# A new order of the first block's side work in a two-layer fp32 kernel

## The reference, cut to what matters

```
feats   = exp(x @ (ab*gs).T - 0.5*|x|^2*ab^2) * AB / sqrt(R)     # random features of 8192 tokens
weights = the same function of input_weights
x1  = layernorm(x + feats @ weights.T)
re  = x1 @ cos(theta + theta_noise);  im = x1 @ sin(phi + phi_noise)
out = layernorm(x1 + sqrt(re*re + im*im))
```

## Time and profile before

| | us |
|---|---|
| median of 3 runs | 774.54 (774.42 to 775.04) |
| the profiled execution | 774.44 |
| its span | 772.6 |
| busy: PE / DVE / ACT / POOL | 750.4 / 496.8 / 373.2 / 179.0 |

### The profile page before, as it was taken

The page is one execution under the profiler, slowest core; times in us unless marked ns, Lnnn a source line. Parts: engine busy times, 40 slices in busy tenths (PEclk is TensorE's granted clock), DMA queues, the critical chain, the costliest instruction groups (busy, mean ns, idle before and its releaser), DMA issues.

```text
span 772.6 us, 10427 instructions
## 1 busy us (share of the span) xinstructions
PE 750.4 (97%) x3396; PEld 617.8 (80%) x3396; DVE 496.8 (64%) x888; ACT 373.2 (48%) x643; POOL 179.0 (23%) x309
## 2 busy tenths in 40 slices
PE   9977989999999999999999999999999999999995
PEld 7855868888888888888888888888888888888884
DVE  4888684847648474674747567474755747576464
ACT  6824926263463616446362644527265462625322
POOL 4966030302112030211203012120201212030222
PEclk9998999999999999999999999999999999999998
DMA  8650050411404032140402214050231405010001
GB/s 277 213 178 0 1 177 1 118 59 46 131 27 149 0 99 78 41 136 21 155 0 79 97 41 136 10 166 1 73 104 41 136 0 162 15 62 6 28 28 54
DMA packets 32750, 60.75 MB, mean 79 GB/s; under 512 B 3168, under 2 KB 3168, under 8 KB 32736
## 3 DMA queue, kind: packets, MB, share of 16 engines
q1 hardware_dynamic: 32736, 60.60, 23.7%
HBM read 43.78 MB, written 16.81 MB: 78 GB/s over the span
## 4 chain that ended last, share of the span: by engine, by line
PE 86%; DVE 7%; ACT 3%; issue 2%; POOL 2%; POOLq 0%; DVEq 0%; ACTq 0%
PE token_ps L502 14%; PE token_ps L504 14%; PE token_ps L503 14%; PE project_ps L491 6%; PE project_ps L493 6%; PE project_ps L492 6%; PE token_ps L554 6%; PE token_ps L552 6%; PE token_ps L553 6%; PE turn_ps L560 3%; DVE stats L730 1%; DVE expo L653 1%; DVE trig L708 1%; DVE trig L712 1%; ACT F_raw L387 1%
## 5 line engine op out<-in xcount | busy, mean ns | idle before, releaser
L306 POOL TENSOR_TENSOR var_eps<-mv,eps 128x1 f32<-128x1 f32 x128 | 41.5, 324 | 568.1 <-DVE mv L734 568.0
L424 ACT ACTIVATE late<-token_ps 128x512 f32<-128x512 f32 x120 | 71.7, 598 | 131.5 <-PE token_ps L504 131.5
L416 ACT ACTIVATE zT_hi<-turn_ps 128x512 fp32r<-128x512 f32 x64 | 38.0, 598 | 182.2 <-PE turn_ps L560 182.2
L491 PE MATMUL project_ps<-xT_hi,gs_hi 128*128 128x512 f32 x248 | 102.1, 412 | 1.0 <-DVE xT_lo L648 0.7
L552 PE MATMUL token_ps<-W_hi,F_hi 128*128 128x512 f32 x256 | 99.7, 389 | 0.0
L554 PE MATMUL token_ps<-W_hi,F_lo 128*128 128x512 f32 x256 | 99.6, 389 | 0.0
L553 PE MATMUL token_ps<-W_lo,F_hi 128*128 128x512 f32 x256 | 99.6, 389 | 0.0
L648 DVE TENSOR_TENSOR xT_lo<-xT_raw,xT_hi 128x512 fp32r<-128x512 f32 x64 | 43.7, 690 | 85.9 <-ACT xT_hi L472 85.5
L493 PE MATMUL project_ps<-xT_hi,gs_lo 128*128 128x512 f32 x248 | 98.0, 395 | 0.0
L492 PE MATMUL project_ps<-xT_lo,gs_hi 128*128 128x512 f32 x248 | 97.4, 393 | 0.0
L745 DVE TENSOR_TENSOR late<-z,late 128x512 f32<-128x512 f32 x64 | 44.2, 691 | 81.9 <-ACT late L457 81.3
(11 more groups left out here) (126 smaller groups left out, 1333.2 us busy)
## 6 DMA issues: line engine op xcount, KB each, us to landing
xT_raw<-in_xT SPq DMA_DIRECT2D x16, 1024.0 KB, 5.9
x_tok<-in_x SPq DMA_DIRECT2D x16, 1024.0 KB, 7.0
out_tokens<-o_tile SPq DMA_DIRECT2D x64, 256.0 KB, 2.0
norm_bc<-token_norms SPq DMA_DIRECT2D x15, 256.0 KB, 3.6
trig<-in_gsT SPq DMA_DIRECT2D x4, 256.0 KB, 4.0
z<-in_wT SPq DMA_DIRECT2D x4, 256.0 KB, 4.7
trig<-in_theta_noise SPq DMA_DIRECT2D x4, 256.0 KB, 6.7
trig<-in_theta SPq DMA_DIRECT2D x4, 256.0 KB, 7.9
```

The costliest lines, as they stand in the source:

```text
L424: nc.scalar.activation(dst, bank[:, :], ACT.Square).then_inc(square_done, 1)
L491: nc.tensor.matmul(o, gs_hi[:, c, cols], rhs_hi[:, c, :], start=(c == 0), stop=False)
```

## The change

GpSimd turns all four tiles of theta and the first of phi ahead of the roots, makes the four roots of block 0 without angle work between them, and turns the second tile of phi behind them. VectorE turns the other two tiles of phi itself, as one tile of double width, and takes over the three sums of squared columns. VectorE splits block 1's columns before it reduces the first two angles. It reduces theta's third and fourth tile between the residuals. ScalarE rounds block 1's columns before it takes the token squares; the third tile's sines come before the first turned tile is rounded, the fourth's after it. At the end of step 0 ScalarE's order is written out, with the four token squares of block 3 last.

```diff
@@ GpSimd
-            a = squares[1]
-            pool.wait_ge(squares_made, C + 2)
-            pool.tensor_tensor(a[0], a[0], a[1], ALU.add).then_inc(block_squares_summed, 1)
...
-            for c in range(3):
-                add_noise(trig, c, theta_loaded, HALF_PI)
-                take_turns(trig, c)
+            for c in range(C):
+                count_turns(trig, c, theta_loaded, HALF_PI)
+            count_turns(late, 0, phi_loaded, 0.0)
...
                 if first:
-                    take_turns(late, 0)
-                    for c in range(1, C):
-                        add_noise(late, c, phi_loaded, 0.0)
-                        take_turns(late, c)
+                    count_turns(late, 1, phi_loaded, 0.0)
@@ ScalarE
+            act.wait_ge(project_done, 2 * C)
+            split_hi(1)
             act.wait_ge(columns_cleared, 1)
             act.wait_ge(x_loaded[1], 16)
             for j in range(C):
                 sum_square(2, j, 1, 0)
-            act.wait_ge(project_done, 2 * C)
-            split_hi(1)
...
-            for c in (0, 1):
+            for c in (0, 1, 2):
                 sine(trig, c, cos_hi, 0)
...
                     round_turned(0)
+                    sine(trig, 3, cos_hi, 0)
                     round_turned(1)
-                    sine(trig, 2, cos_hi, 0)
-                    sine(trig, 3, cos_hi, 0)
...
+                if first:
+                    square(0, 1)
+                    square(1, 1)
+                    magnitude(0)
+                    magnitude(1)
+                    round_columns(0)
+                    square(2, 1)
+                    magnitude(2)
+                    round_columns(1)
+                    square(3, 1)
+                    magnitude(3)
+                    round_columns(2)
+                    round_columns(3)
+                    for j in range(C):
+                        sum_square(b + 3, j, slot, 1 - slot)
+                    return
@@ VectorE
+            a = squares[1]
+            dve.wait_ge(squares_made, C + 2)
+            tt(a[0], a[0], a[1], ALU.add).then_inc(block_squares_summed, 1)
+            dve.wait_ge(squares_made, 2 * C)
+            tt(a[2], a[2], a[3], ALU.add).then_inc(block_squares_summed, 1)
...
+                if n == 1:
+                    dve.wait_ge(block_squares_summed, 2)
+                    tt(a[0], a[0], a[2], ALU.add).then_inc(block_squares_summed, 1)
...
+            def whole_angles(cs):
+                angle, turns = late[:, cs, :], late[:, slice(C + cs.start, C + cs.stop), :]
...
+                tt(angle, angle, turns, ALU.add).then_inc(angle_step, 1)
+                ts(turns, angle, 1.0 / (2 * np.pi), ROUNDER, ALU.mult, ALU.add).then_inc(angle_step, 1)
+                ts(turns, turns, -ROUNDER, -TWO_PI_A, ALU.add, ALU.mult).then_inc(angle_step, 1)
+                tt(angle, angle, turns, ALU.add).then_inc(turns_made, cs.stop - cs.start)
...
+            for c in range(C):
+                split_lo(1, c)
             reduce_angle(trig, 0, 0)
             reduce_angle(trig, 1, 0)
             turn_norms(2, 0)
-            for c in range(C):
-                split_lo(1, c)
...
                     halves(n[j], j, y[:, j % 2, :], y_made, stats, stats_made)
+                    if first and 1 <= j < C - 1:
+                        reduce_angle(trig, j + 1, 0)
...
                 if first:
+                    split_turned(0)
+                norm1(C - 1)
+                if first:
                     exponent(C * (b + 2) + 1, 1, slot, project_ps[1], 1)
                     split_sine(trig, 0, cos_hi, cos_lo, 0, cos_made)
+                    split_sine(trig, 1, cos_hi, cos_lo, 0, cos_made)
                     split_turned(1)
+                    split_sine(trig, 2, cos_hi, cos_lo, 0, cos_made)
+                    reduce_angle(late, 0, C)
                     split_turned(2)
+                    split_sine(trig, 3, cos_hi, cos_lo, 0, cos_made)
                     split_turned(3)
+                    reduce_angle(late, 1, C)
+                    whole_angles(slice(2, 4))
+                    split_sine(late, 0, sin_hi, sin_lo, C, sin_made)
+                    reduce_angle(late, 2, C)
+                    reduce_angle(late, 3, C)
+                    split_sine(late, 1, sin_hi, sin_lo, C, sin_made)
+                    split_sine(late, 2, sin_hi, sin_lo, C, sin_made)
+                    split_sine(late, 3, sin_hi, sin_lo, C, sin_made)
```

## The result

The changed kernel takes 776.44 us (median of 11 runs, 775.54 to 777.97), the kernel before beside it 774.90 (11 runs, 774.42 to 776.22): a ratio of 1.0018, interval [1.0010, 1.0027]. It is slower, as forecast, but by 1.54 us, not by 3.7. The profiled execution has a span of 774.8 us against 772.6.

The account below looks back on a forecast made before the run. Only the opening, one VectorE-ScalarE chain to block 1's first z, was taken to bound the kernel. Tail 4.35 less 0.65 for an earlier last sine gave +3.7 us: 778.2 us, range 774.2 to 781.2.

Parts of the forecast that it names:

- Piece 3: From the last sine to VectorE's last xT_lo: ScalarE's token squares coming last make it 4.35 us later, 1 either way.
- Rival (b): Tail wait hidden, sums of squares slipping in while ScalarE waits for VectorE: total about +1 us, 775.6; chance 0.12.
- Piece 2: From VectorE's first residual to the last sine: less contention and undelayed roots, leaving the last sine 0.65 us earlier than before.
- My 3.9 for the double-width steps: VectorE's four steps on two phi tiles as one, before the last sine: 3.9 us taken, between 2.1 and 4.4.
- The term of 2.8 for GpSimd's one tile: Between first residual and last sine, GpSimd's one remaining tile delays VectorE: four instructions at 0.7 us, 2.8 in all.
- excess of 0.7: Extra us for a VectorE instruction with two SBUF inputs beside GpSimd's work: 1.3 instead of 0.61.
- Piece 1: VectorE up to its first residual: contention with GpSimd's earlier start makes it 5.3 us late, bounds 0 and 9.
- The signs that I had named: Right: splits end near 18.8, last sine near 76.7, block 1's first transpose near 108.5; wrong: last sine before 74.
- Rival (a): The front wins: GpSimd waits at most turns, excess 0.35 for 14 instructions, last sine 71.2, total 773.3; chance 0.15.
- The clock: TensorE's 1.2 GHz stretch after longer idle before block 1's later matmuls: taken as costing 0, bounds 0 and +2 us.
- TensorE's two long waits: TensorE idle 4 to 5 us before its first transpose and about 4 before block 2's projection, the former off the chain.
- The idle after 115: TensorE, once past the opening: no idle after 115 us, named as a sign of being right.

## Why the direction was right and the size wrong

**The bound** was right: only the opening moves the time. From block 1's last transpose on (116.69 before, 118.78 after) the rest of the span is 655.9 to 656.0 us in the kernel before, the changed kernel and all eight experiments: each gain or loss is made ahead of that transpose. All but one were there already at the last xT_lo; only with the transpose moved was what had been gained up to that point lost behind it.

**Piece 3, the tail,** was right: forecast 4.35, measured 4.20, and 4.18 in the kernel before with only this edit. The wait in front of the transpose was expected at about 3 us and is 2.71. It was worked out from program order and durations of the earlier trace rows alone. Rival (b) falls with it: ScalarE waits for the sums (2.34 and 2.40) with the token squares behind them in its list.

**Piece 2 is where the forecast failed most, by the price of contention.** I made it 29.6 us from the first residual to the last sine; it took 28.34. My 3.9 for the double-width steps is what they took (66.69 to 70.61):

```profile
66.69 1.22 DVE L725 TENSOR_TENSOR late<-late 128x1024 f32<-128x1024 f32 x1
67.94 0.69 DVE L728 TENSOR_SCALAR late<-late 128x1024 f32<-128x1024 f32 x1
68.67 0.69 DVE L731 TENSOR_SCALAR late<-late 128x1024 f32<-128x1024 f32 x1
69.47 1.22 DVE L734 TENSOR_TENSOR late<-late 128x1024 f32<-128x1024 f32 x1
```

The estimate by pages of the Trainium skill that I set beside them comes to 3.8, not to the 3.9 that I wrote.

The term of 2.8 for GpSimd's one tile, four instructions at an excess of 0.7, was too large. Only three places beside it stretch, by 0.96 (z, 0.55 alone), 0.41 (two cosine splits, 1.29 alone) and 0.50 (one, 0.68 alone), 1.9 in all, so 0.9 of the error. Another 0.5 is the four rounds of residual, statistics and normalise, which without the stretched z took 7.6 us, not 8.1:

```profile
57.35 1.51 DVE L760 TENSOR_SCALAR z<-y,mv,rstd 128x512 f32<-128x512 f32 x1 [0.36 <-POOL rstd L295]
...
59.45 1.70 DVE L643 TENSOR_TENSOR cos_lo<-trig,cos_hi 128x512 fp32r<-128x512 f32 x2
...
61.67 1.18 DVE L643 TENSOR_TENSOR cos_lo<-trig,cos_hi 128x512 fp32r<-128x512 f32 x1
```

**Piece 1** had the same fault and a smaller error: 5.3 late forecast, 4.57 measured (31.60 less 27.03, each from the first split). The five instructions that follow the first split cost 5.94 − 0.61 = 5.33 us, 1.07 each, not the 1.3 that I took. So VectorE was 1.8 us late behind the loop of exponents and splits, not 2.8. Block 1's splits then took 5.45 against 5.2, and the angle pairs 3.93, inside my 3.2 to 4.2. What I got wrong is that the price has no one value: it goes with what GpSimd has in flight. GpSimd's timeline beside the five:

```profile
15.31 1.79 POOL L270 TENSOR_TENSOR trig<-trig 128x512 f32<-128x512 f32 x1 [2.58 <-DMA trig<-in_theta]
17.18 0.94 POOL L274 TENSOR_SCALAR trig<-trig 128x512 f32<-128x512 f32 x1
18.21 0.93 POOL L277 TENSOR_SCALAR trig<-trig 128x512 f32<-128x512 f32 x1
19.22 0.93 POOL L280 TENSOR_SCALAR trig<-trig 128x512 f32<-128x512 f32 x1
```

Both engines step by the same 1.02 there (GpSimd starts at 17.18, 18.21, 19.22, VectorE's sums at 18.58, 19.60 and the exponents at 20.61). Beside a GpSimd sum (1.3 alone) one VectorE instruction comes to 1.7, as the third sum at 21.93.

Together pieces 1 and 2 erred by 0.7 + 1.3 = 2.0 us and piece 3 by 0.15, which is, to rounding, the distance from +3.7 to +1.52. So the mechanism stood, and the term that failed is the excess of 0.7 us for each contended instruction: it was 0.46 for the five behind the first split, and 1.9 us in place of 2.8 in all beside the one tile of piece 2.

The signs that I had named say the same. The splits' end (18.66), the first residual (46.27) and the transpose's wait came. The last sine (74.61) is 2.1 before 76.7, the last xT_lo came at 101.16 and not from 102.5 on, and block 1's first transpose at 106.97 and not near 108.5. The last sine missed the sign of being wrong, before 74, by 0.6.

**Rival (a)** named this direction. Its cause, a smaller excess, was partly so; but the last sine came 2.7 earlier, not 5.5, and the tail kept its price. The Trainium skill states the mechanism in SBUF — State Buffer, section "SBUF: two separate sides": an exclusive lock, held for a whole instruction. The trace agrees in that one engine's instruction holds up the other's, both ways (GpSimd's tensor_scalar takes 0.93 beside VectorE, 0.62 undisturbed). That the lock lasts for the whole instruction it doesn't show: a VectorE sum (0.61 from start to start alone) and a GpSimd tensor_scalar (0.62), one after the other, would step by 1.23, and they step by 1.02.

**The clock** was put at nothing, and that held: 0.50 in 101:103 came while VectorE's rounds still led, and from 105 the clock was full, ahead of the transpose at 106.97. TensorE's two long waits came about as forecast and cost nothing by themselves (5.46 us before its first transpose, 4 to 5 expected; 4.63 before block 2's projection, about 4 expected). That it can be paid, the profiled run with the transpose behind the last split shows.

**The idle after 115** was forecast as none, and there is none; but the wait of 1.9 us for an exponent at 112.71 I had not listed, and from the z to block 1's last transpose it is 12.4 us both times (104.30 to 116.69, 106.37 to 118.78). Before, TensorE filled that wait with matmuls at 1.2 GHz; now it did them at full clock and stood waiting for VectorE.

## What to carry to other kernels

Before work is moved off an engine, look at what stands behind the last item of each other engine's list: a tiny instruction (here a transpose of 0.2 us) that waits for it holds up all that its own engine has queued, and small work that nobody is waiting for goes into the places where its engine would wait anyway. Where GpSimd and VectorE both read SBUF, count what GpSimd does as VectorE's time too: price each VectorE instruction by the GpSimd instruction in flight (1.02 us a step beside a tensor_scalar, up to 1.7 beside a sum, 0.61 alone), and expect a later start of GpSimd's work to move a good part of the collisions (here 0.9 of 1.5 us). When two halves of a change lie on one chain with opposite signs, run each half alone first. And ask of such a tiny instruction who else waits for it: moved behind the last split, the transpose held back a store and, through it, VectorE.

## What the runs showed of the hardware

GpSimd's six turned tiles, 28 instructions and some 32 us of its busy time (167.7 against 135.9), cost VectorE's chain 9.5 us. Only some instructions pay: sums, splits, angle steps, and the normalise too (0.55 to 1.51), which has one tensor input; a VectorE tensor_scalar went from 0.43 to 0.72 and 1.40. Exponents with an input in PSUM took 0.71 to 0.75 where they stand alone, beside GpSimd or not.

GpSimd's start put off by 1.9 us, counted from the first split (2.58 behind it in place of 0.64), took 1.5 us from the splits, and 0.9 of them came back on later instructions. And the slow clock came or stayed away at one and the same place: behind idle times of 2.10 and 1.87 us the same twelve project matmuls ran at 1.2 GHz from their seventh on in one kernel, and at 2.4 GHz throughout in the other. In the one where the clock fell, TensorE had also stood idle for 0.86 us ahead of the four transposes in front of that wait; in the other it had worked without a gap from 106.97 to 110.84.
